# Moving the softmax-sum chain of two attention layers from SyncE's queue to GpSimd's program, with two score buffers, a later reload and a two-part projection

## The reference, cut to what matters

```python
qkv = x.reshape(b, h * w, c) @ qkv_w.T + qkv_b            # 12 heads of 16
attn = einsum('bnqd,bnkd->bnqk', q, k) * scale + bias     # bias: rel_h[..., :, None] + rel_w[..., None, :]
attn = softmax(attn, axis=-1)                             # 196 x 196 for each head
out = einsum('bnqk,bnkd->bnqd', attn, v)
return out @ proj_w.T + proj_b
```

## Time and profile before

| | us |
|---|---|
| median of 3 runs | 1823.75 (1820.84 to 1829.52) |
| the profiled execution, its own time | 1811.68 |
| its span in the trace | 1809.9 |
| granted TensorE clock, mean over the span | 0.76 of full |
| main loop of `l1`, first S to the first matmul of the projection | 641.3 to 914.2 |
| main loop of `l3`, likewise | 1485.5 to 1754.8 |

### The profile page before, as it was taken

The page is one execution under the profiler, slowest core; times in us unless marked ns, Lnnn a source line. Parts: engine busy times, 40 slices in busy tenths (PEclk is TensorE's granted clock), DMA queues, the critical chain, the costliest instruction groups (busy, mean ns, idle before and its releaser), DMA issues. The chain is left out here.

```text
span 1809.9 us, 49953 instructions
## 1 busy us (share of the span) xinstructions
PE 1472.4 (81%) x19107; PEld 1159.2 (64%) x19107; DVE 1142.1 (63%) x4110; ACT 815.1 (45%) x1779; POOL 418.2 (23%) x643
## 2 busy tenths in 40 slices
PE   4868888888876877878877989899988797887878
PEld 4757777777765755656524667688874685565542
DVE  7877777777788555656625684544436655665641
ACT  3633333333345545655503433555552555564530
POOL 2712222222244100000101210566650310000010
PEclk9955555555558898988955589999995798898885
DMA  3000000000002596678425303422325567668812
GB/s 87 1 20 5 4 4 4 4 4 4 4 21 88 156 274 147 165 157 166 87 57 153 115 14 145 133 83 85 95 79 148 173 152 243 164 163 164 174 33 58
DMA packets 80158, 173.57 MB, mean 96 GB/s; under 512 B 18490, under 2 KB 49874, under 8 KB 77428
## 3 DMA queue, kind: packets, MB, share of 16 engines
q1 hardware_dynamic: 74548, 157.52, 34.0%
q0 software_dynamic: 5376, 12.85, 2.3%
HBM read 97.78 MB, written 67.12 MB: 91 GB/s over the span
## 5 line engine op out<-in xcount | busy, mean ns | idle before, releaser
L514 PE MATMUL gru_ps_r<-gru_hp,gru_wp 128*128 128x16 f16 x3920 | 199.9, 176 | 68.0 <-DVE gru_hp L489 68.0
L1294 DVE TENSOR_REDUCE l_ps<-l_ps 98x4 f32<-98x784 f32 x192 | 187.1, 974 | 85.7 <-PE l_ps L1097 85.1
L514 PEld LDWEIGHTS gru_ps_r<-gru_hp,gru_wp 128*128 128x128 f16 x3920 | 150.6, 106 | 88.4 <-DVE gru_hp L489 88.4
L514 PE MATMUL gru_ps_n<-gru_hp,gru_wp 128*128 128x16 f16 x3920 | 191.2, 174 | 0.0
L1236 ACT ACTIVATE l_arena<-l_ps 2x392 fp32r<-2x392 f32 x192 | 93.9, 489 | 191.4 <-PE l_ps L1106 190.8
L1039 POOL TENSOR_TENSOR l_arena<-l_arena,l_arena 128x784 f32<-128x784 f32 x24 | 44.4, 1850 | 515.2 <-DMA l_arena<-rec 500.4
L1243 ACT ACTIVATE l_arena<-l_ps 98x784 f32<-98x784 f32 x192 | 158.1, 824 | 4.6
L1118 PE MATMUL l_ps<-l_arena,l_arena 128*98 128x196 f32 x768 | 124.4, 288 | 37.1 <-ACT l_arena L1236 37.1
L580 ACT ACTIVATE gru_reset<-gru_ps_r,gru_unscale 128x32 f32<-128x32 f32 x196 | 56.3, 287 | 216.5 <-PE gru_ps_r L514 216.5
L514 PEld LDWEIGHTS gru_ps_n<-gru_hp,gru_wp 128*128 128x128 f16 x3920 | 150.0, 104 | 0.0
L1118 PEld LDWEIGHTS l_ps<-l_arena,l_arena 128*98 128x98 f32 x768 | 93.8, 181 | 85.8 <-ACT l_arena L1236 66.6
(11 more groups left out here) (374 smaller groups left out, 4034.8 us busy)
## 6 DMA issues: line engine op xcount, KB each, us to landing
l_arena<-qk SPq DMA_DIRECT2D x96, 294.0 KB
qk<-l_arena SPq DMA_DIRECT2D x48, 392.0 KB, 6.1
rel<-l_arena SPq DMA_DIRECT2D x24, 686.0 KB
l_arena<-rel SPq DMA_DIRECT2D x48, 343.0 KB
qk<-l_arena SPq DMA_DIRECT2D x12, 784.0 KB, 8.7
l_arena<-in_experts_dram SPq DMA_DIRECT2D x8, 1152.0 KB, 7.4
l_arena<-x SPq DMA_DIRECT2D x24, 294.0 KB, 7.2
l_arena<-rec SPq DMA_DIRECT2D x96, 49.0 KB, 2.7
```

The costliest lines, as they stand in the source:

```text
L514: last = pe.matmul(out[:, b, B * m:B * m + B], wp[:, wi, g, m, :], hp[:, b, part, B * k:B * k + B], start=False, stop=True, skip_group_che ...
L1294: dve.tensor_reduce(m, ps[:TH, S_BANK:S_BANK + 2, :TB].rearrange("p c (h k) -> p c h k", h=2), AXIS.X, ALU.max).then_inc(mx_ready, 1)
```

## The change

- **GpSimd's program** issues `store_sums`, `load_sums`, `store_reciprocals`, `load_spread` and `pack` itself, in order of h, around its multiplication. For each h: store sums, wait until they have landed, load them, wait for VectorE's reciprocals, store these, broadcast them (4 DMAs), wait, multiply. `pack` follows for h = 0, 1 after h = 5, for 2 to 4 after 6, for 5 to 7 after 7, and then for each h after itself. A pack of the last two head pairs is now 8 DMAs, not 4, since odd tiles go to rows 64 to 127. So 1 + 1 + 1 + 4 DMAs for each h, and 8, 12, 12, 8, 8, 8, 8 more after h = 5 to 11.
- **Two score buffers**: S has two pairs of banks (S_BANKS), T has one. `mt` has two slots. LAG is 5. TensorE's order in a step becomes S(i), T(i-3), rel, W, X(i-1); ScalarE's becomes exponential, copy of X, rel. The reciprocals of h stand at step 17 + 8h instead of 15 + 8h.
- **Late reload**: the input comes back at steps 80 to 94 instead of 51 to 79.
- **Two-part tail**: the projection first multiplies the first 128 rows for four tiles, which needs four head pairs, and then the last 64, two tiles side by side, one from rows 0 to 63 and one from rows 64 to 127. It uses eight banks.

```diff
@@ gpsimd
+                def store_sums(h):
+                    pool.wait_ge(o_kept, 4 * h + 4)
+                    pool.dma_start(sums_dram[h]..., o_stage[h // 2][HD:128:32, ...]).then_inc(sums_stored, 16)
+                def load_sums(h):
+                    pool.wait_ge(sums_stored, 16 * (h + 1))
...
+                    pool.dma_start(sums[:, :], sums_dram[h]...).then_inc(sums_in, 16)
+                def store_reciprocals(h):
+                    pool.wait_ge(rec_ready, h + 1)
+                    pool.dma_start(rec_dram[h]..., sums[:, :]).then_inc(rec_stored, 16)
+                def load_spread(h):
+                    pool.wait_ge(rec_stored, 16 * (h + 1))
...
+                    for j in range(4):
+                        pool.dma_start(spread[32 * j:32 * j + HD, h % 2, :], row).then_inc(spread_in[h % 2], 16)
...
                 for h in range(2 * PAIRS):
-                    pool.wait_ge(spread_in[h % 2], 64 * (h // 2 + 1))
-                    pool.wait_ge(o_kept, 4 * h + 4)
-                    pool.wait_ge(sums_stored, 16 * (h + 1))
-                    pool.tensor_tensor(o, o, spread[:, h % 2, :], ALU.mult).then_inc(divided, 1)
+                    store_sums(h)
+                    load_sums(h)
+                    store_reciprocals(h)
+                    load_spread(h)
+                    pool.wait_ge(spread_in[h % 2], 64 * (h // 2 + 1))
+                    pool.tensor_tensor(eighth(h), eighth(h), spread[:, h % 2, :], ALU.mult).then_inc(divided, 1)
+                    for done in {5: (0, 1), 6: (2, 3, 4), 7: (5, 6, 7)}.get(h, (h,) if h > 7 else ()):
+                        pack(done)
@@ tensor
                 for i in range(IMAGES + LAG):
                     if i < IMAGES:
                         logits_by_query(i)
-                    if 1 <= i <= IMAGES:
-                        maxima_to_rows(i - 1)
+                    if 3 <= i <= IMAGES + 2:
+                        logits_by_key(i - 3)
                     if i in rel_of_step:
                         rel(rel_of_step[i])
                     if i >= LAG and (i - LAG) % 2 == 1:
                         weigh_values((i - LAG) // 2)
                     if 1 <= i <= IMAGES:
-                        logits_by_key(i - 1)
+                        maxima_to_rows(i - 1)
...
+                for half in range(2):
+                    pe.wait_ge(packed[0][half], 64 * 4)
+                    for n in range(4 * half, 4 * half + 4):
+                        project_first(n)
+                    pe.wait_ge(packed[1][half], 128 * 2)
+                    for n in range(4 * half, 4 * half + 4, 2):
+                        project_last(n)
@@ scalar
-                for i in range(IMAGES + 2):
+                for i in range(IMAGES + 3):
+                    if i >= 3:
+                        g = i - 3
+                        act.wait_ge(t_summed, g + 1)
...
                     if 1 <= i <= IMAGES:
                         act.wait_ge(x_ready, i)
                         act.activation(q[0:2, ...], ps[64:66, R_BANK, :TB]..., ACT.Copy).then_inc(x_copied, 1)
...
                     if i in rel_of_step:
                         rel(rel_of_step[i])
@@ vector
-                    if i >= 15 and i % 8 == 7 and (i - 15) // 8 < 2 * PAIRS - 1:
-                        reciprocals((i - 15) // 8)
+                    if i >= 17 and i % 8 == 1:
+                        reciprocals((i - 17) // 8)
```

More of the change, by code:

```diff
@@ L817, in attention_layer @@
         sums_stored, sums_in, rec_ready, rec_stored = (s.sem(n) for n in "sums_stored sums_in rec_ready rec_stored".split())
-        spread_zero, spread_in, divided, packed = s.sem("spread_zero"), [s.sem("spread0_in"), s.sem("spread1_in")], s.sem("divided"), [s.sem("packed0"), s.sem("packed1")]
+        spread_zero, spread_in, divided = s.sem("spread_zero"), [s.sem("spread0_in"), s.sem("spread1_in")], s.sem("divided")
+        packed = [[s.sem(f"packed_rows{block}_half{half}") for half in range(2)] for block in range(2)]
         y_summed, added, stored = (s.sem(n) for n in "y_summed added stored".split())
@@ L917, in load @@
                     sp.dma_start(dst[row:row + rows, :, cols].bitcast(f32), src[:, :, cols].bitcast(f32)).then_inc(quarter_in[part], 16)
[L919 to L955, removed]
                 def main_step(i):
@@ new lines, in pack @@
+                def pack(h):
+                    p, half = divmod(h, 2)
+                    if h == 0:
+                        pool.wait_ge(rel_stored, 64 * QUADS)
+                    pool.wait_ge(divided, h + 1)
+                    for j in range(4):
+                        e, head = divmod(j, 2)
+                        row = 32 * (p % 4) + HD * head
+                        to = o_full[p // 4][:, half * N // 2:(half + 1) * N // 2].rearrange("r (c o e t) -> r c o e t", c=2, o=2, e=2)[:, :, :, e, :]
+                        of = eighth(h)[32 * j:32 * j + HD, :].rearrange("r (c o t) -> r c o t", c=2, o=2)
+                        if p < 4:
+                            pool.dma_start(to[row:row + HD], of).then_inc(packed[0][half], 16)
+                        else:
+                            for odd in range(2):
+                                pool.dma_start(to[64 * odd + row:64 * odd + row + HD, :, odd, :], of[:, :, odd, :]).then_inc(packed[1][half], 16)
@@ L1096, in logits_by_query @@
                             queries = slice(b * T + half * TH, b * T + (half + 1) * TH)
[L1097 removed]
+                            last = pe.matmul(ps[:TH, S_BANKS[g % 2] + head, half * T:half * T + T], q[:, head, queries], k[:, head, keys],
                                              start=True, stop=True)
@@ L1105, in maxima_to_rows @@
                     for n in range(4):
-                        last = pe.matmul(ps[64:66, R_BANK, n * TH:n * TH + TH], mt[:TH, n, :], ones_at[:TH, :], start=True, stop=True)
+                        last = pe.matmul(ps[64:66, R_BANK, n * TH:n * TH + TH], mt[:TH, g % 2, n, :], ones_at[:TH, :], start=True, stop=True)
                     last.then_inc(x_ready, 1)
@@ L1117, in logits_by_key @@
                             keys = slice(b * T + half * TH, b * T + (half + 1) * TH)
-                            last = pe.matmul(ps[:TH, T_BANK + 2 * (g % 2) + head, half * T:half * T + T], k[:, head, keys],
+                            last = pe.matmul(ps[:TH, T_BANK + head, half * T:half * T + T], k[:, head, keys],
                                              q[:, head, queries], start=True, stop=True)
```

118 lines of the change are left out of this document (59 added, 59 removed).

## The result

The changed kernel takes 1913.66 us in the median (1907.92 to 1916.12, four runs) against 1823.38 for the kernel before in the same session: a ratio of 1.0505, 95% interval 1.0468 to 1.0543. It is slower by 90 us, where the prediction said 97. The profiled execution has a span of 1911.5 us and a mean granted clock of 0.738.

The account below looks back on a forecast made before the run. GpSimd's serial chain was taken to bound the changed kernel: 313.8 us to the reciprocals of h = 10 plus a 58.9 tail, 372.7 a layer against 324.4, 97 us more for two layers. Forecast 1921 us, range 1880 to 1975.

Parts of the forecast that it names:

- The cause: GpSimd's serial order from one head's reciprocals to the next takes 17.05 us, 25.85 or 30.25 with packs, holding up VectorE.
- the signs named: VectorE waits over 9 us from h = 6, GpSimd issues of 1.1 us unbroken, multiplications 26 to 30 us apart.
- Issue of a DMA: On GpSimd, each plain DMA was put at 1.1 us to issue, with 0.5 and 1.25 as the ends.
- rival A: GpSimd issues cost 0.5 us and landings 2.0, so the kernel gets faster, 1771 us; chance 0.15.
- five packed cycles: GpSimd's cycles with packs, from the reciprocals of h = 5 to those of h = 10: 138 us.
- Landing: Each dependent DMA of GpSimd's chain lands in 2.8 us; four landings a cycle, 11.2 us.
- Rival C: Landings are longer under load, 3.7 us, with issues of 1.25: 97 us a layer more, 2018 us; chance 0.15.
- First stretch: Main loop from a layer's first S to the reciprocals of h = 5: 175.8 us.
- The tail: From the reciprocals of h = 10 to the layer's end: 58.9 us against 66.3 before, TensorE waiting for the last pack.
- The second score buffer: Ordinary steps fall to a mean of 1.76 us, 0.3 less, worth nothing where GpSimd's cycle exceeds eight steps.
- The moments in `l1`: They fall between the projection's parts, under TensorE.
- The base: Two layers, 97 us longer, added to the profiled 1811.7 us make 1909; the runs' median lies 12 above, so 1921.

Follow-up runs that it names:

- Both kernels that isolate the chain: Changed kernel with the sums, reciprocals, broadcasts and repacks back on SyncE: 1828.12 us; kernel before with only these moved to GpSimd: 1911.04 us.
- grouped projection: Kernel before with only the projection's matmuls reordered, eight of 128 rows then eight of 64, in eight banks: 1775.63 us, ratio 0.9752.
- tail-alone kernel: Kernel before with only the two-part tail added, the sums-to-repacks chain staying on SyncE: 1781.91 us, ratio 0.9776.

## Why the prediction was right, step by step

**The cause held.** GpSimd's serial chain decides, with VectorE standing before the reciprocals and TensorE behind it. Both kernels that isolate the chain say so, 86 and 91 us of the 90 measured. Of the signs named, VectorE's waits are there, 16 in all and up to 16.1 us, though one of 14 us comes as early as h = 1, and an ordinary step is as short as forecast. The multiplications of `l3` behind h = 5 stand 24.6, 24.4, 31.2, 17.5 and 17.4 us apart, not 26 to 30, and the row of issues of 1.1 us isn't there.

**Issue of a DMA: 1.1 assumed, 0.50 to 0.61 measured** (the broadcasts' mean is 0.495 us, the repacks' 0.518 and 0.515, the sums' store 0.614). The plain DMA costs GpSimd half of its indirect one, and about what it costs SyncE. By this term alone rival A was right: by its issues of 0.5 and landings of 2.0 the five packed cycles would have been 84 us. It wasn't reached because the next term was wrong the other way.

**Landing: 2.8 for each, measured 1.9 to 3.8 with DMA shares up to 0.53 and 5 to 9.6 with more, from bulk loads.** One number for two cases, with the issue at twice its price beside it, were the failing steps, here and not in the cause. Rival C had the mechanism, but took a uniform 3.7; the mean of the 48 stores is 4.1.

**First stretch, 175.8 forecast to the reciprocals of h = 5, 201.1 measured in `l3`,** from its first S at 1547.43. Step 12 came at 41.1 (39.3). Steps 12 to 17 and what follows to h = 0 took 29.9 (27.0): the strided steps with W at 5.7 and not 4.85, for the lower clock. The cycle from h = 0 to 1 took 27.1 and not 17.05, its store landing beside the loads in 8.35. From h = 2 to 4 it was 61.1 (58.3), of which the seven cheap `rel` steps before step 40 took 22.9 (19.5). From h = 4 to 5 it was 25.0 for 17.05, by a store that landed in 8.5 us and broadcasts that GpSimd waited 7.95 for. With h = 1 to 2 as forecast (16.8), that is 25.3 too long.

**The five packed cycles, 138 forecast, 115.3 measured** (24.5, 24.6, 28.2, 20.6 and 17.3). By their cheap issues and landings of 2.0 they would have been 16 to 18. The first three have one or two landings of 5 to 8 us, and the fourth still one of 5.0, beside the reload of the layer's input. Only the fifth, with the loads over, is near rival A's figure.

These two misses cancel: the reciprocals of h = 10 stand at 316.3 and were forecast at 313.8. The total was right for a sum of two wrong terms of opposite sign, so the closeness of 1921 to 1914 says less than it seems.

**The tail, 58.9 forecast, 47.7 measured.** The miss is the issue term again. TensorE was to start on the last eight matmuls, when the last repacks have landed, 47.2 us after the reciprocals of h = 10, and it starts at 1898.79, 35.0 after them: 21 issues on that path at 0.59 less each make 12.4 us. From there to the end it took 12.7 us (11.7). The matmuls were mis-sized too, with little effect. They had been put at 1.53, read off as if it were their price. That is what they take alternating at the lower clock. In the new order eight of 128 rows need 5.51 us at the full clock, and the eight of 64 rows pair:

```profile
1865.92 7.01 PE L1183 MATMUL l_ps<-l_arena,l_arena 128*96 128x392 f32 x16
1879.45 4.44 PE L1190 MATMUL l_ps<-l_arena,l_arena 64*96 64x392 f32 x16 [6.52 <-DMA l_arena<-l_arena]
1883.82 5.51 PE L1183 MATMUL l_ps<-l_arena,l_arena 128*96 128x392 f32 x16
1898.79 5.00 PE L1190 MATMUL l_ps<-l_arena,l_arena 64*96 64x392 f32 x16 [9.46 <-DMA l_arena<-l_arena]
```

The 64-row groups took 4.44 and 5.00 us, at granted clocks of 0.64 and 0.57 over just these stretches, against 6.2 forecast for the lower level. Unpaired at 1.31 each they would be 10.5, an estimate from the grouped projection's first matmuls, so they do pair. TensorE waits 6.52 and 9.46 us for repacks: the tail is bound by GpSimd's chain, as forecast, and its shorter TensorE work is mostly hidden there. In the tail-alone kernel, where the chain isn't late, the gain is there: its four groups take 20.7 us of TensorE in `l3`, where the kernel before took 49.

**The second score buffer** does what was said of it (ordinary steps of 1.29 and 2.15, mean 1.72 for 1.76 forecast), but what it saves goes into waiting for the chain. With the chain on SyncE and X ahead of `rel` the kernel takes 1797, and without the second buffer and its order of steps 1775: nothing here speaks for having it.

**The moments in `l1`** were put under TensorE. Half of them aren't: four tiles' moments occupy VectorE from 996.03 to 1001.8 in front of the last additions, 5.8 us on the path, a small miss.

**The base.** From the first row maxima to the last addition `l1` grew by 38 us and `l3` by 40, not 48. (The prediction has the two layers before as equal within 2 us; by its table they differ by 3.6.) The span grew by 101.6, and 22 of these lie between the last addition of `l1` and the first row maxima of `l3`, where the profiled execution of before was short: 521.7 us, against 544.0 in the changed kernel and 534 to 550 in the other twelve profiles. The forecast came to 97 by 48 for each layer; the medians differ by 90, of which the layers give 78. What the other 12 us are isn't shown, and that they make up for layers forecast too long is luck.

## What to carry to other kernels

A DMA that another instruction waits for is to be costed at two prices, one for quiet DMA engines and one for those filled with bulk loads; which of them holds is read from the DMA share over the very stretch in which it lands. Moving a dependent chain to another engine's program doesn't give it DMA engines of its own, and written round after round there it becomes serial where SyncE's order interleaved two rounds. And a stretch in which TensorE is always busy at 0.50 of its clock isn't full: ask first what order its matmuls are in, since that was the only part of this change that made the kernel faster.

## What of the hardware was unexpected

- Fp32 matmuls with 128 and with 64 rows in turn kept TensorE at the 1.2 GHz level for 49 us without idle time, 1.53 to 1.6 us for each. Eight and eight grouped ran at 2.4 GHz but for the first 3 us and took 12.43 us for the first sixteen and 10.94 for the second, 0.78 and 0.68 each, over the same banks and with the same data.
- A store of reciprocals behind twelve repacks of the same queue landed in 2.04 us with the DMA share at 0.29, and one behind eight in 7.46 with the share at 0.94. The queue's length mattered little, the load of the DMA engines much.
- A plain DMA costs GpSimd 0.50 to 0.61 us of issue, as a rule without a gap to the next; an indirect one 0.94 and 0.30.
- At the full clock a matmul of 64 rows behind one of 128 stood 0.27 us after it, and one of 128 behind one of 64 stood 0.37, where two of 128 stand 0.18 apart.
